# A recurrence with one difference instead of two, and PSUM banks dealt out anew among experts, receptance and output projection

## What is computed

```python
xn = _layernorm(x)
k, v = mix_k(xn) @ W_k.T, mix_v(xn) @ W_v.T     # mix: x * m + x_prev * (1 - m)
r = sigmoid(mix_r(xn) @ W_r.T)
def step(carry, kv):                            # over the 256 tokens
    aa, bb, pp = carry; k_t, v_t = kv
    ww = u + k_t
    p = max(pp, ww)
    e1, e2 = exp(pp - p), exp(ww - p)
    wkv_t = (e1 * aa + e2 * v_t) / (e1 * bb + e2 + 1e-09)
    ww2 = w + pp
    p2 = max(ww2, k_t)
    e1b, e2b = exp(ww2 - p2), exp(k_t - p2)
    return (e1b * aa + e2b * v_t, e1b * bb + e2b, p2), wkv_t
s = (r * wkv) @ W_o.T
# mixture of 8 experts, each token goes to the nearest centroid
h = rms_norm(xn) @ up_w[e]; a, g = split(h)
y = (a * silu(g)) @ down_w[e] + xn
x = x + s * silu(y)
```

## Time and profile before

| | us |
|---|---|
| median of 3 runs (1302.33 to 1307.1) | 1303.05 |
| profiled execution, its own time | 1303.33 |
| its span in the trace | 1301.3 |
| TensorE busy | 1141.3 (88%) |
| VectorE busy | 1052.4 (81%) |
| ScalarE busy | 812.2 (62%) |
| GpSimd busy | 596.9 (46%) |

### The profile page before, as it was taken

How to read it: one execution, slowest core, us unless ns; L and a number is a source line. 1 busy time by engine, 2 the same in 40 slices (tenths; PEclk the granted TensorE clock), 3 DMA queues, 4 the chain that set the end, 5 groups by cost and what they waited for, 6 DMA issues and landing times. The chain is left out here.

```text
span 1301.3 us, 30853 instructions
## 1 busy us (share of the span) xinstructions
PE 1141.3 (88%) x9562; PEld 782.3 (60%) x9563; DVE 1052.4 (81%) x2450; ACT 812.2 (62%) x1730; POOL 596.9 (46%) x1017
## 2 busy tenths in 40 slices
PE   3766379999971789999999999999999999999995
PEld 2655257666650456666666666666666666666652
DVE  6788979999985588888888888888888878888871
ACT  3555357777760256667666767676667666776663
POOL 4586757776772333334334443444343434343310
PEclk9566689999995699999999999999999999999997
DMA  9511111111110332232223222332233222322310
GB/s 257 146 42 36 36 36 48 45 45 45 46 40 21 83 78 61 72 89 72 65 73 87 73 65 72 80 80 65 72 82 78 65 73 76 84 65 70 75 35 10
DMA packets 147952, 89.23 MB, mean 69 GB/s; under 512 B 73057, under 2 KB 137057, under 8 KB 147553
## 3 DMA queue, kind: packets, MB, share of 16 engines
q1 hardware_dynamic: 143712, 78.92, 23.7%
q0 software_dynamic: 4096, 8.53, 2.3%
HBM read 55.91 MB, written 31.47 MB: 67 GB/s over the span
## 5 line engine op out<-in xcount | busy, mean ns | idle before, releaser
L1398 DVE TENSOR_REDUCE bm<-PS 128x16 f32<-128x1024 f32 x256 | 312.4, 1221 | 58.7 <-PE PS L1750 58.0
L1621 ACT ACTIVATE PT<-PS 128x1024 f32<-128x1024 f32 x256 | 262.4, 1025 | 97.8 <-PE PS L1762 97.8
L1772 PE MATMUL PS<-PT,V 128*32 128x256 f32 x2048 | 137.7, 386 | 0.0
L1875 PE MATMUL PS<-Vf,PTr 128*128 128x65 f32 x1024 | 127.9, 278 | 0.0
L1875 PEld LDWEIGHTS PS<-Vf,PTr 128*128 128x128 f32 x1024 | 119.1, 191 | 13.5 <-issue 13.5
L1602 ACT ACTIVATE PTr<-PS 128x1024 f32<-128x1024 f32 x64 | 65.6, 1024 | 86.8 <-PE PS L1860 86.8
L1762 PE MATMUL PS<-QS,KS 51*128 51x256 bf16 x1024 | 99.7, 273 | 6.3 <-ACT PT L1621 4.6
L1233 POOL CAST parts<-rest 128x512 bf16<-128x512 f32 x32 | 19.6, 611 | 186.6 <-DVE rest L1379 186.6
L1750 PE MATMUL PS<-KS,QS 48*128 48x256 bf16 x1024 | 99.5, 272 | 4.2 <-DVE bm L1398 4.2
L1219 POOL TENSOR_TENSOR zt<-zt,S 128x256 f32<-128x256 f32 x32 | 23.2, 726 | 169.7 <-DVE zt L1318 169.7
L1420 DVE TENSOR_REDUCE nmf<-PS 128x4 f32<-128x1024 f32 x64 | 78.1, 1221 | 19.7 <-PE PS L1833 19.7
(11 more groups left out here) (248 smaller groups left out, 2814.9 us busy)
## 6 DMA issues: line engine op xcount, KB each, us to landing
wsel<-in_qkv_w SPq DMA_DIRECT2D x128, 96.0 KB, 2.5
parts_dram<-parts SPq DMA_DIRECT2D x32, 384.0 KB
QS<-parts_dram SPq DMA_DIRECT2D x64, 96.0 KB
KS<-parts_dram SPq DMA_DIRECT2D x64, 96.0 KB
xs_dram<-zero_t SPq DMA_DIRECT2D x1, 4752.0 KB, 26.7
xs_t<-xs_dram SPq DMA_DIRECT2D x72, 66.0 KB, 1.8
ys_dram<-ys_t SPq DMA_DIRECT2D x72, 64.0 KB, 1.6
QS<-parts_dram SPq DMA_DIRECT2D x64, 64.0 KB
```

What stands on the lines that cost most here:

```text
L1398: dve.tensor_reduce(bm[:, i // 2, :, 2 * (i % 2):2 * (i % 2) + 2, :].rearrange("p q r b -> p r q b"), bS.rearrange("p (r q b k) -> p r q b ...
L1621: act.activation(PT[i % 4][:, :, :], bT.rearrange("p (r k) -> p r k", r=2), ACT.Exp).then_inc(s_exp, 1)
L1772: last = pe.matmul(bC[j * VC:(j + 1) * VC, 0:SEQ], V2[q][:, kt, 4 * g + j, :], PT[(2 * g + j // 2) % 4][:, j % 2, kt * SEQ:(kt + 1) * SEQ] ...
L1875: last = pe.matmul((bF1, bF2)[i][:, at:at + RD + 1], PTr[i][:, j, kt * SEQ + qt * P:kt * SEQ + (qt + 1) * P], Vf[q % 2][:, kt, 2 * i + j, ...
```

## The change

- VectorE forms one difference, d = k - pp, with one subtraction, where it formed two, (pp + w) - k and (k + u) - pp. The tile is half as large.
- ScalarE makes the four arguments of the exponential with four rectifications of 256 columns, each with a bias read from a column (w, -w, u or -u), where it made them with two rectifications of 512 columns without bias. `minus_cols` holds the negated columns; one more instruction in VectorE's set-up fills it.
- The rectifications leave `exps` and become `rectify`, which ScalarE runs behind `experts` T0. `keep` moves from before `experts` T1 to behind it.
- `psX` becomes two banks, 2 and 7, used in turn: TensorE waits for the copy of tile t - 2 instead of t - 1.
- `psR` moves into the second half of bank 5, whose first half is `psO`. Two waits on TensorE keep the two apart: the receptance of sequence t waits for `keep` of t - 2 (which has the same step s), and the output projection of t waits for the tanh of t + 1 (that of the step before).

```diff
-        diff = two("diff", [P, 2, SEQ])
+        diff = two("k_minus_max", [P, SEQ])
-        psU, psX, psH, psY, psO, psKV, psR = PS[0:2], PS[2], PS[3], PS[4], PS[5], PS[6], PS[7]
+        psU, psX, psH, psY, psO, psKV, psR = PS[0:2], PS[2:8:5], PS[3], PS[4], PS[5], PS[6], PS[5][:, SEQ:2 * SEQ]
+        def most(t):
+            return min(t, B) if isinstance(t, int) else t
+                dve.tensor_scalar(ncols[:, :], cols[:, 0:2], -1.0, None, ALU.mult)
-                dve.scalar_tensor_tensor(diff[q % 2][:, 0, :], pp[:, 0:SEQ], cols[:, 0:1], k, ALU.add, ALU.subtract)
-                dve.scalar_tensor_tensor(diff[q % 2][:, 1, :], k, cols[:, 1:2], pp[:, 0:SEQ],
-                                         ALU.add, ALU.subtract).then_inc(s_args, 1)
+                dve.tensor_tensor(diff[q % 2][:, :], k, pp[:, 0:SEQ], ALU.subtract).then_inc(s_args, 1)
-            def exps(t, q):
+            def rectify(t, q):
                 act.wait_ge(s_args, t + 1)
                 after(act, s_ex, t)
-                act.activation(args[:, :, 0, :], diff[q % 2][:, :, :], ACT.Relu, scale=-1.0)
-                act.activation(args[:, :, 1, :], diff[q % 2][:, :, :], ACT.Relu).then_inc(s_relu, 1)
+                d = diff[q % 2][:, :]
+                act.activation(args[:, 0, 0, :], d, ACT.Relu, bias=ncols[:, 0:1])
+                act.activation(args[:, 0, 1, :], d, ACT.Relu, scale=-1.0, bias=cols[:, 0:1])
+                act.activation(args[:, 1, 0, :], d, ACT.Relu, scale=-1.0, bias=ncols[:, 1:2])
+                act.activation(args[:, 1, 1, :], d, ACT.Relu, bias=cols[:, 1:2]).then_inc(s_relu, 1)
+            def exps(t, q):
...
-                    act.copy(xsT[q % 3][:, :], psX[:, 0:P]).then_inc(s_xsT, 1)
+                    act.copy(xsT[q % 3][:, :], psX[q % 2][:, 0:P]).then_inc(s_xsT, 1)
...
                 experts(quad, p, 0)
                 take(0)
+                if runs(e[0]):
+                    rectify(*e)
+                take(1)
                 if runs(b[0]):
                     keys_values(*b)
-                take(1)
+                experts(quad, p, 1)
                 if runs(k[0]):
                     keep(*k)
-                experts(quad, p, 1)
                 take(2)
                 if runs(e[0]):
                     exps(*e)
...
             def receptance(t, q):
                 after(pe, s_th, t)
+                after(pe, s_s, t - 1)
                 project(t, 2, psR[:, 0:SEQ], s_rp)
             def out_projection(t, q):
                 pe.wait_ge(s_rwkv, t + 1)
                 after(pe, s_s, t)
+                pe.wait_ge(s_th, most(t + 2))
...
-                    after(pe, s_xsT, t)
-                    pe.transpose(psX[:, 0:P], xs_t[q][:, 0:D], ident[:, :]).then_inc(s_fx, 1)
+                    after(pe, s_xsT, t - 1)
+                    pe.transpose(psX[q % 2][:, 0:P], xs_t[q][:, 0:D], ident[:, :]).then_inc(s_fx, 1)
```

More of the change, by code:

```diff
@@ L131, in layer_zero @@
         cols = sb("cols", [P, 5])
+        ncols = sb("minus_cols", [P, 2])
         ommix = sb("ommix", [P, 3])
```

## The result

The changed kernel takes 1320.35 us, median of 4 runs (1315.23 to 1324.68). The kernel before took 1302.69 on the same chip, median of 4 (1300.41 to 1307.1). The ratio is 1.0126, 95% interval 1.0098 to 1.0155: 17.7 us slower, 19.3 were predicted. The profiled executions are 1315.23 us (span 1313.2) and 1303.33 (span 1301.3), 11.9 apart; the profiled one of after is the quickest of its four.

The account below looks back on a forecast made before the run. It took a TensorE-ScalarE ring through the T1 gate (8.90 us), beside a nearly full VectorE, to hold the step. 1303.3 + 20.7 (22 x 0.94) - 1.4 = 1322.6, median 0.3 lower: 1322.3 us, range 1311 to 1332.

Parts of the forecast that it names:

- the ring that the prediction named: TensorE to T0 gate, ScalarE to late keep, back through the receptance: 9.79 us a step against 8.85, 0.94 more.
- 1 to 2 us before one projection in each step, released by keep: Sign expected in the profile after: TensorE idle 1 to 2 us before one L805 each step, released by keep.
- rival "same": Receptance's wait covered, only the ScalarE ring of 9.03 left: +2.6 us, 1306 us; chance 0.08.
- ScalarE ring of 9.03: ScalarE's chain from the T0 gate, closed through TensorE: 8.65 us before, 9.03 with four rectifications replacing two.
- 0.41 from start to start: Each of four rectifications on ScalarE: 0.41 us, 1.64 for four against 1.26 for two; bounds 0.32 and 0.47.
- The new subtraction: VectorE's single difference: 0.70 us taken, between 0.41 and 0.72, replacing instructions of 0.724 and 0.674.
- The intake: Steps 0 to 10, without expert tiles: part of VectorE's saving counts, -1.4 us, between 0 and -5.
- VectorE as the bound: Rival "faster": VectorE bounds the step and both rings are loose, 16.8 us less, 1286 us; chance 0.05.
- Each ring closes to 0.04 us: Argument against VectorE as the bound: each ring closes that nearly, with no VectorE instruction in it.
- the ring through the T1 gate: TensorE to the T1 gate, then ScalarE and back: 8.90 us before, 7.91 with the rectifications moved out.
- The receptance's wait is covered: Rival at TensorE's receptance: its wait for keep costs nothing, +2.6 us, 1306 us; chance 0.08.
- The clock rival: TensorE's idling before the receptance lowers the granted clock in each step: 50 us more, 1372 us; chance 0.07.

Follow-up runs that it names:

- e1: Changed kernel with the PSUM banks and waits of the kernel before, all else as changed: 1301.72 us, ratio to before 0.9984.
- e2: Changed kernel with keep back ahead of experts T1, shared bank and both new waits staying: 1306.87 us, ratio to before 1.0033.
- e7: Changed kernel with the four rectifications without their bias columns: one run of 1314.42 us.
- e5: e4 with the changed kernel's order on ScalarE in the intake, steps 0 to 10: 1281.52 us, ratio to before 0.9818.
- e3: Kernel before with only the single difference and four rectifications, at the old place right ahead of the exponential: 1316.16 us, ratio 1.0101.
- e4: Kernel before with the single difference and four rectifications at the start of ScalarE's step, ahead of experts T0: 1284.05 us, ratio 0.9857.
- e9: Changed kernel, shared bank and late keep included, with the rectifications at the start of ScalarE's step: 1295.67 us, ratio to before 0.9929.
- e10: e9 with keep and the copy of keys and values back ahead of experts T1: 1283.31 us, ratio to before 0.9853.
- e6: Kernel before with only the PSUM edit, two token banks and the shared bank with both waits: 1301.95 us, ratio 0.9978.
- e8: Kernel before with only its two rectifications moved to the start of ScalarE's step: 1298.5 us, ratio 0.996.

## Why the prediction was right, and where not

**The step.** It was forecast at 9.79 us and is 9.84, by the ring that the prediction named: T0 transpose to T0 gate 3.44 against 3.45 measured, T0 gate to the end of keep 3.94 against 3.87, hand-off 0.14 against 0.25 and 0.15 in two steps, receptance to the next T0 transpose 2.27 against 2.38 and 2.35. The last was held as a bound ("a restart of TensorE on each handover 0.12"); it came in every step, 278.34 - 276.93 = 1.41 from the receptance to the up product (1.38 to 1.41 in the others) where the earlier trace rows show 1.30. The receptance starts 7.57 us after the zero, 7.52 predicted. That this ring carries the loss is shown by three runs: e1 and e2 each open it, by the bank or by the place of keep, and the wait at the receptance and 0.76 or 0.45 us a step go; e7 shortens it by 0.37 us and the step by 0.35.

**The waits.** "1 to 2 us before one projection in each step, released by keep" was half right. TensorE idles 0.96 + 0.60 = 1.56 us (0.96 + 0.49 in the next step), but 0.96 of it stand at the transpose ahead, released by the copy of the hidden values. This is the ring through `psH` that e2 made visible. The prediction had the row in its hand (the copy that ends 0.14 before the transpose) and used it only to value the second token bank at nothing. It did not ask what the rectifications do to the same bank one turn later. Without the shared bank the change costs 9.08 a step (e1), and it is this ring that sets it: TensorE waits there at its T2 transposes and not at T0. So the rival "same", with its ScalarE ring of 9.03, and the expectation for e1 had nearly the right number from the wrong ring.

**The rectifications.** 0.41 from start to start was taken, 0.40 measured (four in 1.59, 273.18 to 274.77), length 0.50.

**The new subtraction.** 0.70 us was taken; the group of 180 to 340 us in after has 468 ns:

```profile
L598 DVE TENSOR_TENSOR k_minus_max<-kv,pp 128x256 f32<-128x256 f32 x17 | 8.0, 468 | 1.2
```

and in e5, where VectorE is full, 733 ns:

```profile
L598 DVE TENSOR_TENSOR k_minus_max<-kv,pp 128x256 f32<-128x256 f32 x20 | 14.7, 733 | 1.4
```

The same instruction is 0.27 us shorter in after. It is not that VectorE waits there, since it waits in e3 too, with 731 ns. What differs is what GpSimd has beside it: in after the end of the addition L415 (from 278.21 on, 0.83 long) and the start of the product L402 (279.01) beside a subtraction from 278.83 on (0.50); in e5 the product L408 from 278.21 on (1.12 long) beside one from 278.84 on (0.77). In e2 it is both, 0.49 in one step and 1.22 in the next, where it starts inside GpSimd's product L402, and 860 ns in the mean:

```profile
282.77 1.65 POOL L402 TENSOR_TENSOR ev<-ex,kv 128x512 f32<-128x512 f32 x1
```

```profile
283.48 1.22 DVE L598 TENSOR_TENSOR k_minus_max<-kv,pp 128x256 f32<-128x256 f32 x1
```

So the term was right for e3, e4, e5, e9 and e10 (0.73), too high for after, e1 and e7 (0.46 to 0.47) and too low for e2 (0.86): the order on ScalarE shifts VectorE against GpSimd. In after it was off the path, so nothing of it reached the time. Which GpSimd instruction slows it is read from the coincidence, not from a run made for it.

**The intake.** Forecast -1.4, got -5.8 at step 12. Of the 5.8 us 4.15 are there at the scatter (135.01 against 139.16), the other 1.65 come between it and the scan of step 12 and are not explained. In the 4.15 two causes were mixed. The column "scatter" parts them: 138.7 to 139.5 in the three kernels with two differences; 137.0 to 138.2 in the three with one difference and keys and values ahead of `take(1)` (e3, e4, e10), which is VectorE's part, 1 to 2 us as forecast; and 132.8 to 135.0 in the five where `take(1)` stands ahead of keys and values (after, e1, e2, e7, e9). The prediction passed over that order: `take(1)` holds ScalarE's work for the intake, and it now stands ahead of a copy that waits for TensorE. In before and in after, ScalarE, the same place of the intake:

```profile
66.49 0.59 ACT L692 COPY kv<-PS 128x512 f32<-128x512 f32 x1 [4.46 <-PE PS L806]
```

```profile
66.39 0.59 ACT L696 COPY kv<-PS 128x512 f32<-128x512 f32 x1 [1.52 <-PE PS L817]
```

The copy starts at the same time, but 3 us of the idle time ahead of it are filled. So the size of this part is about 3 us in five of six kernels. In the sixth, e5, it was there up to step 6 and was lost in the one wait of 4.95 us shown above. How the gain builds up is not the same in all of them, either: the scan of step 6 is at 91.26 in after and at 87.4 to 88.0 in e1, e2, e5, e7 and e9. Such waits, with a releaser outside of the profile, are in other profiles too (3.1 us at the same instruction in e10, whose scatter is 1.2 later than that of e4), so a difference of 1 us in this column says little.

**The rivals.** VectorE as the bound fell: a VectorE with 0.6 us less to do and everything else in place gave a step of 9.40 (e3). But its sum, 1286, is about what e4 and e10 reach, once the rings are loosened. "Each ring closes to 0.04 us" was too strong: the ring through the T1 gate closes (8.90 in a step of 8.90), the one through the T0 gate was 8.65, and VectorE's own 8.72 set the first six steps of this stage. "The receptance's wait is covered" fell for this kernel by the row at 276.93 and is true of e6 and e10, where keep is early. The clock rival fell: TensorE idles about 1.5 us in each step, and the granted clock is 1.00 in every stretch of 20 us from 180 to 400. The Trainium skill (TensorE: Matmul & The Clock Gate, section on psum-queue depth-cycling) tells of short idles between matmul groups that make the clock swing; no run here shows it in this stage.

**The PSUM banks.** The rule of the Trainium skill that independent groups of matmuls should go through different banks (Perfetto Trace Analysis, section Matmuls) had a size of 0 to 0.04 us a step for the tokens (e6) and, for the shared bank, of 0 in e6 and e10 and of some 0.7 in e9 and 0.8 in after. What decided was not the bank but where in ScalarE's order the instruction stands that empties it.

**The total.** 22 x (9.84 - 8.85) = 21.8 against 20.7 in the sum, less 5.8 for the intake instead of 1.4, makes 16; the medians differ by 17.7. That the total came within 2 us of the forecast is in part luck, since the intake gave 4.4 more than its term. What is left is in the rest, which no edit touches: over twelve profiles it took 935.7 to 945.5 us. It accounts for 4 of the 6 us by which e3 missed 1310, and with the intake it is why the profiled executions of before and after are only 11.9 apart.

The profiles show what the rest goes with. Add up, over stretches of 20 us from the scan of step 33 on, the time multiplied by what the granted clock lacks to 1.00: 29 us in after and 30 in e8, whose rests are the short 936.7 and 935.7, 35 in before (939.6), 41 in e3 (943.8) and 43 in e7 (945.5), all of it before 460 and behind 1240 us; over the twelve profiles the two quantities correlate with 0.91. The four runs of after have mean granted clocks of 0.942, 0.938, 0.935 and 0.929 with 1315.23, 1320.2, 1320.5 and 1324.68 us. Why the clock rises earlier in one execution than in another, no run shows.

## What to carry to other kernels

An engine at 98% may still not be what holds the step, and here it held only six of 21: write down the ring (out of one engine, down the other's order, back) with its instructions, and see whether the engine you relieve has any of them. Do this for every buffer with a single copy that both engines touch, at its new neighbours in the order, and not only for the wait that the diff adds. A wait added by a shared buffer costs what stands ahead of its releaser in that engine's order: move the releaser forward, or put new work where the engine is idle already, before giving the buffer up; the same work cost 0.55 us a step at one place (e3) and let 0.7 be gained at another (e4).

## What the runs showed of the hardware

- A 256-column subtraction with both inputs in SBUF took 0.42 to 0.50 us at one place beside GpSimd's work, 0.68 to 0.77 at another and 1.22 at a third (e2), with the same work on both engines in the step; an estimate of contention from another place of the schedule can be off by half of the true value (0.70 taken, 0.47 measured).
- TensorE, after an idle of 0.49 to 0.73 us, took 0.07 to 0.11 us more for the receptance and the down product behind it in every step of after, e7 and e9 (1.38 to 1.41 against 1.30 or 1.31 in before and e3), at a granted clock of 1.00. In e1 and e10 some steps show 1.38 to 1.40 with no idle right ahead of the receptance, so the idle is not shown to be the only cause.
- The second layer, the same instructions in all kernels, differed by up to 9.8 us between twelve profiles, together with how long the granted clock stayed under 1.00. Half a per cent of the whole is thus not to be had from a single profile; the distance of two scans inside the first layer gave the same step within 0.01 us in e4, e5 and e10.
